# Message-passing kernel: some TensorE waits left out in the score loop, the value pass and the fused passes, one wait moved to GpSimd, and a zero product cut from 512 to 8 columns

## The reference

```python
# layer 0: dot-product attention with 8 heads, then a feed-forward block
scores = sum(Q[tgt] * K[src], -1) / sqrt(DK)
alpha  = segment_softmax(scores, tgt)
agg    = segment_sum(alpha[:, :, None] * V[src], tgt)
# layer 1: two graph convolutions with edge weights (dense adjacency products)
agg = segment_sum(x[src] * ew[:, None], dst) + x
# layer 2: three GATv2 convolutions (4, 4 and 1 heads)
e_feat = leaky_relu(xl[src] + xr[dst]);  logits = einsum(e_feat, att)
a      = segment_softmax(logits, dst)
out    = segment_sum(xl[src] * a[:, :, None], dst)
# layer 3: one weighted convolution, degree-normalised
x = _layernorm(x + layer(x))      # after each of the four
```

## Time and profile before

| | us |
|---|---|
| median of 3 runs | 6065.07 |
| lowest, highest | 6062.72, 6069.36 |
| the profiled execution, its own time | 6063.98 |
| its span in the trace | 6062.2 |
| of it: score loop | about 194 to 1282 |
| value pass | about 1388 to 1797 |
| fused passes | about 2284 to 3418, 3474 to 4614, 4672 to 5811 |

### The profile page before, as it was taken

How to read it: one execution, slowest core, us unless ns; L and a number is a source line. 1 busy time by engine, 2 the same in 40 slices (tenths; PEclk the granted TensorE clock), 3 DMA queues, 4 the chain that set the end, 5 groups by cost and what they waited for, 6 DMA issues and landing times. The chain is left out here.

```text
span 6062.2 us, 111971 instructions
## 1 busy us (share of the span) xinstructions
PE 4236.7 (70%) x22034; PEld 3503.4 (58%) x22035; DVE 4336.3 (72%) x10827; ACT 2687.3 (44%) x6544; POOL 3638.8 (60%) x3882
## 2 busy tenths in 40 slices
PE   2677777748888985777666567777665677667649
PEld 2566666636664555666666456666664566666634
DVE  5887888877665137777777777777777777777754
ACT  0455555535542002555455435545454345545441
POOL 2777777733320007777777477777774777777720
PEclk7888999979998996666676666666666666776759
DMA  3567777744443853333333133333331333333317
GB/s 83 170 205 214 222 208 214 211 128 122 134 140 105 277 165 95 87 87 89 86 92 89 46 85 92 88 85 88 85 92 40 85 80 85 83 81 82 81 26 263
DMA packets 488021, 725.86 MB, mean 120 GB/s; under 512 B 79979, under 2 KB 306626, under 8 KB 487679
## 3 DMA queue, kind: packets, MB, share of 16 engines
q0 software_dynamic: 123968, 282.81, 19.0%
q1 hardware_dynamic: 236544, 350.89, 18.4%
q10 hardware_dynamic: 127166, 88.94, 4.8%
HBM read 601.60 MB, written 120.75 MB: 119 GB/s over the span
## 5 line engine op out<-in xcount | busy, mean ns | idle before, releaser
L1757 POOL DMA_INDIRECT rows<-scratch_gat,index x2496 | 2523.0, 1011 | 1337.9 <-issue 737.6
L2075 PE MATMUL sums<-xr,hot_t 128*128 x5016 | 1032.0, 372 | 258.8 <-DVE z L1995 218.9
L2075 PEld LDWEIGHTS sums<-xr,hot_t 128*128 128x128 f32 x5016 | 915.0, 273 | 314.4 <-issue 297.3
L2130 PE MATMUL sums<-mix,vhot 128*128 128x128 f32 x4992 | 1092.7, 388 | 1.2 <-issue 0.3
L922 POOL DMA_INDIRECT rows<-scratch_kv,index_ring x832 | 841.0, 1011 | 260.7 <-issue 249.3
L2130 PEld LDWEIGHTS sums<-mix,vhot 128*128 128x128 f32 x4992 | 957.3, 285 | 40.2 <-issue 1.1
L1825 ACT ACTIVATE moved_sums<-sums x624 | 372.7, 597 | 1162.7 <-PE sums L2130 1111.3
L1995 DVE TENSOR_TENSOR z<-sums,rows 128x512 f32<-128x512 f32 x624 | 428.5, 687 | 546.0 <-DMA rows<-scratch_gat,index 499.2
L1815 ACT ACTIVATE vhot<-iota,edge_local 128x128 f32<-128x128 f32 x2496 | 788.7, 390 | 0.0
L1357 PE MATMUL sums<-at_hot,lo_hot 128*128 128x200 f32 x2496 | 572.0, 378 | 4.6
L1981 DVE TENSOR_TENSOR mix<-rows,alpha 128x256 f32<-128x256 f32 x1248 | 471.9, 420 | 68.1 <-PE sums L2130 19.8
(11 more groups left out here) (508 smaller groups left out, 5891.1 us busy)
## 6 DMA issues: line engine op xcount, KB each, us to landing
piece<-scratch_adj SPq DMA_DIRECT2D x90, 1280.0 KB, 6.5
local_ring<-scratch_local_rows SPq DMA_DIRECT2D x159, 512.0 KB
scratch_spool<-rows ACTq DMA_DIRECT2D x208, 256.0 KB
vals<-scratch_spool SPq DMA_DIRECT2D x208, 256.0 KB, 2.6
scratch_adj<-stage SPq DMA_DIRECT2D x25, 1600.0 KB
rows<-scratch_gat,index POOLq DMA_INDIRECT x2496
local_ring<-scratch_local_rows ACTq DMA_DIRECT2D x53, 512.0 KB
mask<-scratch_masks SPq DMA_DIRECT2D x234, 80.1 KB
```

Of the source, the lines that this page charges most:

```text
L1757: eng.indirect_dma_start(rows[:, slot, q, k * LINE:(k + 1) * LINE], None, table, bass.IndirectOffsetOnAxis(ap=index[:, slot, s:s + 1], axis=0)
L2075: ins = eng.matmul(B.ps[:, at + k * D:at + (k + 1) * D], hot_t[:, slot, k * P:(k + 1) * P], queries[:, bass.ds(at_block, D)], start=True, ...
L2130: ins = eng.matmul(B.ps[:, bass.ds(of_block * D, D)], hot[:, v % MIXES, k * P:(k + 1) * P], mix[:, v % MIXES, k * D:(k + 1) * D], start=Fa ...
```

## The change

In the score loop PE's wait for `hots` is gone; the wait for `weighed`, which DVE raises later in its own order, stays. In `sum_up` of the fused passes the wait for `moved` is gone; ACT raises `hot_v` of a group behind that move in its own order. In the value pass two of PE's three waits are gone, those for `halved` and `mixed`; POOL waits for `mixed` before the second remainder instead, so that `split` stands for all three. And the zero product on bank 7 has 8 columns in place of 512.

```diff
@@ score loop, PE
                         ins.then_inc(asked.sem, 1)
-                        eng.wait_ge(hots.sem, hots.at(1) + n)
                         eng.wait_ge(weighed.sem, weighed.at(1) + n)
@@ fused passes, PE, sum_up
                         eng.wait_ge(mixed.sem, mixed.at(RING_PORTIONS * PORTION_GROUPS + 1) + m)
-                        eng.wait_ge(moved.sem, moved.at(1) + m)
@@ value pass, POOL
                         eng.wait_ge(halved.sem, halved.at(3) + n * 3)
+                        eng.wait_ge(mixed.sem, mixed.at(BODY_GROUPS + 1) + n)
                         eng.tensor_tensor(part(q, 2), rest[:, q, :, 0:extra_width], part(q, 1), ALU.subtract
                                           ).then_inc(split.sem, 1)
@@ value pass, PE
-                        eng.wait_ge(halved.sem, halved.at(2) + n * 3)
                         eng.wait_ge(split.sem, split.at(2) + n * 2)
-                        eng.wait_ge(mixed.sem, mixed.at(BODY_GROUPS + 1) + n)
-                        eng.matmul(B.bank(7), B.zeros[:, 0:P], B.zeros[:, :], start=False, stop=True, skip_group_check=True)
+                        eng.matmul(B.bank(7)[:, 0:8], B.zeros[:, 0:P], B.zeros[:, 0:8], start=False, stop=True, skip_group_check=True)
```

## The result

| | before | after |
|---|---|---|
| runs of the comparison, us | 6062.72, 6065.07, 6069.36, 6072.20 | 6026.02, 6027.41, 6201.67, 6202.78 |
| median | 6067.22 | 6114.54 |
| ratio, runs at the upper clock | | 0.993 (0.9914 to 0.9947) |
| profiled execution: its time, span | 6063.98, 6062.2 | 6026.02, 6024.2 |

What follows compares the result with a forecast made beforehand. POOL's gathers were taken to bound the score loop and fused passes, PE with its sequencer the value pass. Savings of 40 + 0.3 = 40.3 us gave 6065.07 - 40.3 = 6024.8, forecast 6025; 8-in-10 range 6012 to 6046.

Steps and rivals of the forecast that it cites:

- the step that carried it: Value pass: two PE sequencer instructions ahead of each group vanish, 0.19 us a group, 208 groups, 40 us less.
- The stops at a turn's head: Value pass: PE's stop for loading block numbers, once in four groups, shrinks from 1.00 to about 0.8 us.
- The fused passes and the score loop: Score loop nothing; fused passes 0.3 us in all, since POOL's gathers bound them; gathers' length 10 us less or 6 more.
- POOL's new wait: Value pass: POOL's wait for `mix` and one more instruction cost nothing, hidden by POOL's lead of 4.1 us.
- The lead: Value pass: how long POOL's result lies ready before PE wants it; it shrinks from 4.1 to 3.5 us.
- The columns: Value pass: 8 columns gain nothing alone; with the sequencer 0.2 us ahead, 512 would cost up to 0.1 a group.
- The clock: Rival: value pass falls to the lower clock, group about 2.1 us instead of 1.74, 75 - 40 us more, 6100; chance 0.04.

Runs made afterwards that it cites:

- E1: Kernel before with PE's value-pass waits for `halved` and `mixed` gone, POOL waiting for `mixed`, 512 columns kept: median 6027.1 us, ratio 0.9929.
- E4: Changed kernel with the value pass's wait for `mixed` back on PE and gone from POOL: ratio to before 0.9963 at the upper clock; three more runs 6195 to 6201.
- E3: Kernel before with only the waits for `hots` (score loop) and `moved` (fused passes) left out, value pass untouched: ratio 1.0009.
- E6: Changed kernel with PE's value-pass loop over eight groups a turn instead of four: 7740.9 us once, 7856 to 7884 five times, beside 7778 before (another chip).
- E5: Changed kernel without the value pass's zero product: 7699.3 us once, 7866 to 7879 five times, beside 7778 before (another chip).
- E2: Kernel before with only the value pass's zero product cut to 8 columns, all waits kept: 6194.3 to 6197.9 us, ratio 1.021.
- E9: Kernel before with 8 columns in the zero product and an added 512-column one behind each group's third fp32 product, all waits kept: ratio 1.0002.
- E8: Kernel before with 256 columns in the value pass's zero product, all waits kept: 7772 to 7796 us beside 7778 before (another chip), ratio 1.0005.
- E11: Changed kernel with 512 columns kept in the value pass's zero product: median 6035.6 us beside 6081.0 before, ratio 0.9931.
- E12: Kernel before with the value pass's waits left out, 512 columns kept, sixteen groups a turn on PE: 7679.1 to 7691.8 us beside 7755.8, ratio 0.9904.

## Why the prediction was right, and what it missed

**The time.** 6025 was forecast, and the executions at the upper clock took 6026 and 6027. The median of all four runs, 6114.5, lies far outside the 6012 to 6046 that was given; that the execution that was profiled was a short one was luck, since six of ten were long. For the short ones, the step that carried it held: PE's sequencer set the pace of the value pass, and each of its instructions ahead of a group cost about 0.1 us though its wait was long over. I took 0.19 us a group; the trace has 1.74 - 1.54 = 0.20 inside a turn and 1.96 - 1.76 = 0.20 with the stops. The stops at a turn's head are 0.84 us (41.8 in 50), near 0.8 as forecast. E1 has this gain from the waits alone, E4 gives 0.074 of it back for one instruction.

**The fused passes and the score loop.** Nothing was forecast, and E3 measured 1.0009 with an interval that holds 1. The gathers stayed between 1093 and 1098 us, inside the ends that the earlier trace rows gave.

**POOL's new wait.** Hidden, as forecast, but for the first group of the pass, where there is no lead yet: the idle time ahead of its zero product grew from 0.14 to 0.82 us. That is under a microsecond, once. The lead shrank more than the prediction said: at the median of the 208 groups POOL's last remainder now ends 2.9 us before the zero product starts, where 3.5 were forecast and 4.1 measured before. POOL's operations had also become longer (last section), which the prediction left out.

**The columns, the step that failed.** The prediction said that once the sequencer is 0.2 us ahead, 512 columns "would stand in the way", up to 0.1 us a group, and that this edit takes the cost away. There was no such cost: E1 and the changed kernel have the same group on average, 1.76 us. I had compared one gap, 0.22 against 0.18, and not asked whether the pair behind it has room to make up for it. It has: 0.27 in place of 0.35.

**The clock, a rival whose chance and price were both wrong.** It got 0.04. It came in six of ten executions. The reason against it was that PE would have fewer pauses. E6 has half the stops and was low in six of six runs, E5 has a step and a product less and was low in five of six, and once the clock is down PE is busy all the time and it stays down; so few pauses are no protection. What the runs tell apart is the zero product: 8 columns with all waits, always low (E2); the same with 512 columns put elsewhere in the group, 256, and the change with 512, never a long run (E9, E8, E11). Over everything on record, none of the 58 executions of the kernel before and none of the 46 of the versions with 256 or 512 columns was long; of the 32 with 8 columns or none, 23 were long and one, E6's first, fell inside the pass. A busy share of records doesn't show this: an 8-column product counts as 0.17 us busy and a 512-column one as 0.38. The clue was in the prediction's own sentence "The 512 columns were work, though of zeros", and I gave it no weight. The price was mis-sized too. I read 2.1 us a group from four fp32 products of the fused pass, 2.07 us, which left 0.03 for the four bf16 products between them and the zero product together. At the lower level a pair takes 0.64 us, so a group is 2.56 to 2.58, and the whole pass costs 125 us more than before, not 75. Nor do the 40 us come off again, as the prediction had it: the array is the bound then, and the change's long runs (6201 to 6218) are no shorter than E2's, which keeps all waits (6194).

So the prediction was right about the execution that was profiled, and wrong as advice: over its ten executions the changed kernel averages 6136 us, 0.9 to 1.1% slower than before, where its chance of being slower was put at 0.04.

**What set off the falls.** Four falls inside a pass were caught, and each came soon behind a stop of PE at the head of a turn. These are the first zero products behind those stops, with the idle time before them, in E2, E6 and twice in E12:

```profile
1405.88 0.18 PE L2720 MATMUL sums<-zeros 128*128 128x8 bf16 x1 [0.82 <-ACT parts L2671]
2115.54 0.18 PE L2718 MATMUL sums<-zeros 128*128 128x8 bf16 x1 [0.89 <-POOL rest L2682]
2082.94 0.39 PE L2720 MATMUL sums<-zeros 128*128 128x512 bf16 x1 [1.40 <-POOL parts L2688]
2162.03 0.39 PE L2720 MATMUL sums<-zeros 128*128 128x512 bf16 x1 [1.44 <-POOL parts L2688]
```

The first product that takes longer starts at 1407.85, 2117.30, 2084.23 and 2162.57, at most 2.0 us behind. A turn of E12 lasts some 26 us, so that both of its falls lie there is hardly chance. It fits that a stop can set off a fall and that the columns decide whether the level comes back: one fall is then enough for E6, however rare its stops are. No run here takes the stops out, so this is argued and not shown.

**What stays open.** Why one execution of the changed kernel stays at the upper level and the next doesn't, and why most stops are followed by no fall. The fall can come 18 us into the pass (E2) or after 272 us (E6), and the level can stay down from the start (E5).

## What to carry to other kernels

When an engine seems to wait, look whether the data was really late; if it lay ready for microseconds, the sequencer's own instructions may be the bound, as here, where leaving out a wait that another one implies was worth 0.07 to 0.1 us each time. Before shrinking or dropping a TensorE product that costs nothing, ask what it does for the clock: here a zero product of 512 columns was free, and with 8 columns or none the pass fell to half the clock, or stayed there, in 24 of 32 executions. When the runs of a kernel fall into two groups, look at the clock of each stage before calling one group a disturbance, and judge the change by all of its runs.

## What the runs showed of the hardware that I had not expected

**A level that stays.** In E2, E5 and E6 PE ran without a pause at 0.50 of the clock for 515, 530 and 121 us, and the level didn't rise before the pass was over. The Trainium skill ("TensorE: Matmul & The Clock Gate", section "🎯 Why this matters for your kernels") advises to keep TensorE continuously busy to get to the upper level; by that rule these passes should have come up early on, and the measurement decides: a full row of busy records was not enough here.

**POOL's small operations stretch beside DVE.** POOL's first remainder took 0.41 us on average before and takes 0.63 now, the second 0.26 and 0.46, for 36 columns as ever. The timeline of the changed kernel shows when:

```profile
1599.61 0.69 DVE L887 TENSOR_TENSOR vhot<-iota,edge_local 128x512 f32<-128x512 f32 x1 [1.11 <-PE sums L2723]
1600.01 0.40 POOL L2682 TENSOR_TENSOR rest<-extra,parts 128x36 f32<-128x36 bf16 x1 [0.71 <-ACT parts L2669]
...
1601.77 0.74 DVE L2703 TENSOR_TENSOR mix<-vals,extra 128x512 f32<-128x512 f32 x1
...
1601.92 0.70 POOL L2682 TENSOR_TENSOR rest<-extra,parts 128x36 f32<-128x36 bf16 x1
...
1603.31 0.74 DVE L2703 TENSOR_TENSOR mix<-vals,extra 128x512 f32<-128x512 f32 x1
...
1603.46 0.70 POOL L2682 TENSOR_TENSOR rest<-extra,parts 128x36 f32<-128x36 bf16 x1
```

Where it starts just behind DVE's product it ends 0.11 us after DVE does, at 1602.62 behind 1602.51 and at 1604.16 behind 1604.05, as if it had waited for it; the one at 1600.01 began halfway through DVE's one-hot and ends 0.11 us behind that, at 1600.41 behind 1600.30. The Trainium skill ("SBUF — State Buffer", section "🔬 SBUF: two separate sides") says that a DVE operation with two SBUF inputs and a GpSimd operation that reads SBUF exclude each other, and that the first to start holds on to the end; these rows agree with that, with up to 0.45 us a time. With POOL idle for 41% of the pass it cost nothing. No run here took it apart.
